# GpSimd's sums of probability tiles: one instruction of four heads in place of one for each head

## The reference, cut to what matters

```
x1 = x  + out_proj(causal block-masked attention(layernorm(x)))
x2 = x1 + out_proj(attention(layernorm(x1), ctx))      # ctx: 4 x 1024 x 512
y  = x2 + W2 relu(W1 layernorm(x2))
attention: p = softmax(q k^T * scale); out = p v
```

## Time and profile before

| | |
|---|---|
| median of 3 runs | 3573.18 us (3571.24 to 3574.4) |
| profiled execution, span | 3571.7 us |
| PE / DVE / ACT / POOL busy share | 92% / 59% / 37% / 51% |
| additions L974 in `e_` | 640 of 128x512, mean 1280 ns |
| additions L974 in `b_` | 384 of 128x128 to 128x512, mean 920 ns |
| products L1019 | 256 in `e_`, 128 in `b_` |
| self attention `b_` | about 612 to 1345 us |
| cross attention `e_` | about 1661 to 2650 us |

### The profile page before, as it was taken

One profiled execution on the slowest core, in us unless ns is written; L12 is line 12 of the kernel. 1 busy time (PEld: TensorE's weight loads), 2 busy tenths in 40 slices (PEclk: granted clock), 3 DMA queues, 4 the chain that ended last, 5 costly groups with the idle time before them and its releaser, 6 DMA issues. The chain is left out here.

```text
span 3571.7 us, 54829 instructions
## 1 busy us (share of the span) xinstructions
PE 3303.2 (92%) x18570; PEld 2078.1 (58%) x18570; DVE 2124.1 (59%) x2949; ACT 1323.5 (37%) x2369; POOL 1826.2 (51%) x1552
## 2 busy tenths in 40 slices
PE   7969997999999996969999999999968499999999
PEld 6857884545454545754444444444427388888887
DVE  4435545777777765757998989899948611111110
ACT  2112221545455552223665656566642221111111
POOL 3124332444444455644887878788876362222222
PEclk9979996999999998987999999999989799999999
DMA  5535446343444405534332423324026631111110
GB/s 195 177 118 195 170 162 152 83 89 79 88 96 96 96 14 179 214 131 104 73 69 52 93 49 72 74 52 93 10 77 233 250 95 48 51 49 51 50 48 24
DMA packets 211665, 361.36 MB, mean 101 GB/s; under 512 B 16312, under 2 KB 92600, under 8 KB 207312
## 3 DMA queue, kind: packets, MB, share of 16 engines
q1 hardware_dynamic: 211408, 358.01, 35.2%
HBM read 214.20 MB, written 142.61 MB: 100 GB/s over the span
## 5 line engine op out<-in xcount | busy, mean ns | idle before, releaser
L974 POOL TENSOR_TENSOR e_probs<-e_probs 128x512 f32<-128x512 f32 x640 | 799.2, 1280 | 234.6 <-ACT e_probs L1064 228.8
L1064 ACT ACTIVATE e_probs<-e_st 128x512 f32<-128x512 f32 x1024 | 603.4, 597 | 428.5 <-PE e_st L1132 369.6
L997 DVE TENSOR_REDUCE e_neg_max<-e_nat 128x1 f32<-128x1024 f32 x512 | 615.1, 1214 | 92.9 <-PE e_nat L1110 67.1
L974 POOL TENSOR_TENSOR b_probs<-b_probs 128x128 f32<-128x128 f32 (+2 forms) x384 | 341.7, 920 | 427.7 <-ACT b_probs L1064 427.7
L1064 ACT ACTIVATE b_probs<-b_st 128x512 f32<-128x512 f32 (+3 forms) x768 | 367.2, 491 | 419.1 <-PE b_st L1136 331.2
L997 DVE TENSOR_REDUCE b_neg_max<-b_nat 128x1 f32<-128x128 f32 (+7 forms) x512 | 369.5, 751 | 184.0 <-PE b_nat L1114 180.1
L1132 PE MATMUL e_st<-e_qs,e_ks 99*128 99x512 f32 x1024 | 464.0, 459 | 10.4 <-issue 7.6
L1363 DVE CAST m_hid_hi<-m_hid 128x512 fp32r<-128x512 f32 x128 | 59.1, 462 | 599.1 <-ACT m_hid L1315 599.1
L1342 POOL TENSOR_TENSOR m_hid_lo<-m_hid,m_hid_hi 128x512 fp32r<-128x512 f32 x128 | 165.1, 1290 | 461.5 <-DVE m_hid_hi L1363 461.5
L1132 PEld LDWEIGHTS e_st<-e_qs,e_ks 99*128 99x128 f32 x1024 | 192.9, 190 | 339.4 <-ACT e_probs L1064 233.2
L1110 PE MATMUL e_nat<-e_ks,e_qs 96*128 96x512 f32 x1024 | 351.6, 429 | 27.0 <-DVE e_neg_max L997 15.5
(11 more groups left out here) (195 smaller groups left out, 5815.2 us busy)
## 6 DMA issues: line engine op xcount, KB each, us to landing
b_qs<-sq_hi SPq DMA_DIRECT2D x30, 512.0 KB, 7.4
b_ks<-sk_hi SPq DMA_DIRECT2D x30, 512.0 KB, 14.3
e_qs<-cq_hi SPq DMA_DIRECT2D x30, 512.0 KB, 6.6
e_ks<-ck_hi SPq DMA_DIRECT2D x30, 512.0 KB, 14.5
d_x<-in_ctx SPq DMA_DIRECT2D x8, 1024.0 KB, 6.3
ck_hi<-d_part_hi SPq DMA_DIRECT2D x32, 256.0 KB, 5.7
ck_lo<-d_part_lo SPq DMA_DIRECT2D x32, 256.0 KB, 5.9
cv<-d_tok_out SPq DMA_DIRECT2D x32, 256.0 KB, 5.4
```

The lines of the kernel that those rows point to most:

```text
L974: last = pool.tensor_tensor(here, here, there, ALU.add)
L997: dve.tensor_reduce(neg_max[:, u:u + 1], nat[:, bank_of[u]:bank_of[u] + banks, 0:keys // banks], AX.XY, ALU.max, negate=True).then_inc(max ...
L1064: act.activation(probs[:, (p * NS + k) % PR, j, first:TOK], st_ps[:, blk % 2, first:TOK], ACT.Exp).then_inc(exped, 1)
```

## The change

The loop over the four heads goes; one instruction takes the four heads of both tiles as 128 x 4 x width operands. Where the width is 512, these are 2048 columns in a row; elsewhere four runs with a stride of 512. The semaphores waited for and raised are the same. The groups, their order and all other engines' programs stay.

```diff
-                            for j in range(HG):
-                                here, there = (probs[:, (p * NS + i) % PR, j, first:TOK] for i in (k, k + more))
-                                last = pool.tensor_tensor(here, here, there, ALU.add)
-                            last.then_inc(added, 1)
+                            here, there = (probs[:, (p * NS + i) % PR, :, first:TOK] for i in (k, k + more))
+                            pool.tensor_tensor(here, here, there, ALU.add).then_inc(added, 1)
```

## The result

The changed kernel takes 4225.05 us (median of 4 runs, 4207.81 to 4244.95) against 3573.79 us before: 1.1825 times the time, 95% interval 1.1788 to 1.1863. That is 651 us slower. The direction was forecast; 3849 us and the range's upper end of 3980 were too low by far.

What follows compares the result with a forecast made beforehand. TensorE's queue was taken to bound the kernel, with VectorE next. 3573 + 208 (cross attention waits) + 40 (self attention waits) + 28 (lower clock) = 3849 us; eight-in-ten range 3655 to 3980.

Steps and rivals of the forecast that it cites:

- GpSimd's own time: Additions in attention: one 4 x 512 instruction takes 4.6 us, about 0.4 us sooner per tile; at most 6 us gained.
- The wait of VectorE's product: VectorE's product waits for the running GpSimd instruction's end; the longest wait is one instruction, rising from 1.28 to 4.6 us.
- two operands: VectorE operations with two SBUF inputs contend with GpSimd for one port pair, held for the whole instruction.
- The waits in `e_`: Cross attention: VectorE's late maxima stall TensorE, 13 us a body, 208 us for 16, bounds 77 and 285.
- my worst case: Cross attention: all six bursts of a body caught early, products 32.3 us a body, a body 17.8 us longer.
- the slip after single bursts: Cross attention: after a one-instruction burst, VectorE's product starts before the next burst; half a body loses 5.5 us, not 8.6.
- The waits in `b_`: Self attention: products take up to 9 us more a body; TensorE loses 2.5 a body, 40 us, bounds 0 and 144.
- mostly absorbed: Self attention: VectorE's 12 us idle a body and TensorE's lead of up to four units take most added product time.
- The clock: Cross attention: stalls drop TensorE to 1.2 GHz for 14 us, costing at most 7 us a spell; 28 us in all.
- The third rival: The clock falls in every cross attention body: 112 us in place of 28, total 3933 us, up to 4030; chance 15%.

Runs made afterwards that it cites:

- the one-operand run: Changed kernel with VectorE's product replaced by a second reciprocal in place, one SBUF operand, normalisation left out: 3568.91 us, ratio to before 0.9998.
- the runs: Kernel with wide additions in cross attention only, self attention as before: 4009.69 us, ratio 1.1231; 213 us of the 651 left for self attention.
- after: The changed kernel with wide additions in both attention stages, against the kernel before: 4225.05 us, 1.1825 times the time.
- The filled kernel: Changed kernel plus bf16 matmuls of 512 columns on zeros where TensorE stalls, in both attention stages: 4096.47 us, ratio 1.1476.

## Why the prediction was right in direction and wrong in size

- **GpSimd's own time**: right. 4.55 us of mean against 4.60, and hardly anybody waits for it: 3.0 us in cross attention.
- **The wait of VectorE's product**: right, to 0.1 us in the single wait, and by the one-operand run it carries the whole loss. The cause is wider than "two operands": the constant multiplication waits too.
- **The waits in `e_`**: TensorE's idle time grew by 247 us, where I had 208 with bounds of 77 and 285. That it came so near is in part luck, since two parts of the working were wrong. I counted one catch for each GpSimd instruction with a product 2.84 us behind the last; the step with two pieces puts the second one straight into the second instruction, 4.07 us where I had 1.8, and TensorE stalls 6.50 us where I had 2.4 + 0.8. The sum of the products is 532.8 us, 33.3 a body, where I had 400 in all; even my worst case, 32.3 a body, is 517. I also counted on the slip after single bursts, and it hardly occurs: 105 of the 256 products last 3.75 to 4.25 us, and there are 96 bursts and 16 second pieces to catch them.
- **The waits in `b_`**: right. TensorE's idle time there grew by 44 us where I had 40, while the products grew from 71.8 to 158.5 us: "mostly absorbed" held. Self attention is longer by 202 us all the same (213 by the runs), because TensorE is busy 158 us more for the same 5648 matmuls. I had written that growth by over 80 us would show that the slack isn't where the products wait. It doesn't show that; I had given `b_` no term for the clock at all.
- **The clock**: this is the step that failed. I wrote "One in four bodies, 4 x 7 = 28 us", and no row stood behind "one in four". TensorE's busy time at an equal count of matmuls grew by 348 us, 189 in cross attention and 158 in self attention. The idle time grew by 286 us, where 208 + 40 = 248 were forecast for waits. I had seen the low clock only behind stalls of 2.46 us and longer, at the loop's boundaries, and priced it as a rare event. In after it follows most stalls of 1.7 to 2.2 us as well, and these come several times a body, so its price is of the size of the stalls themselves. The third rival's sign came true, a granted clock below 0.9 in `e_` (0.81). Its price for it did not: one spell a body, 112 us.
- How exactly 634 us divide isn't settled. 348 and 286 are what the records say, and a slow matmul can also fill time that would have been a wait. The filled kernel is 129 us faster while VectorE's waits are no shorter, so I take the clock's part to be at least that.

## What to carry to other kernels

Before joining GpSimd instructions, look at the longest and shortest duration of VectorE's small SBUF instructions beside them: where the long ones end with GpSimd's, their wait grows with GpSimd's instruction, whatever is saved in starts. Where such a wait reaches TensorE, price two terms and not one: the stall, and the matmuls behind it at half the clock, for each stall that recurs (here it was so behind 47 of 62). The cure here was to give the contending operation to GpSimd itself (0.5% below before). Placing it earlier in VectorE's queue took back 461 of the 651 us.

## What the runs showed of the hardware that was not expected

- A VectorE multiplication of 64 float32 columns with a constant, SBUF to SBUF, waited up to 4.33 us for GpSimd, as the product of two tensors did (4.26); a reciprocal in the same place took 0.55 us each time.
- TensorE's granted clock fell to about 0.5 behind stalls of 2.06 us, and in the body of self attention shown behind stalls of 1.71 and 1.92 us; behind one of 1.82 us in cross attention it stayed at 1.00. 16 x 84 added matmuls on zeros, less 16 left out in the first body, 1328 in all, took 129 us off the changed kernel's time.
- A matmul of 512 float32 columns with 32 columns of weights, 8 in a row on one quarter of the array, cost 0.89 us each, one of bf16 on the whole array 0.20 (272 us / 1328).
